# A two-layer graph network on one core: setup reordered with larger batches and two-byte compares, both node stages in five pieces, and the last stage's biases by a matmul

## The reference

```python
def reference(x, src, dst, edge_attr_128, edge_weight, kernel0, bias0, W_fwd, b_fwd, W_back, b_back, gamma, beta):
    h = relu(layernorm(x))
    # layer 0: a degree-normalised sum over edges, times a matrix
    deg = segment_sum(w, src) + 1; dinv = rsqrt(deg)
    x = x + relu(segment_sum(dinv[src] * w * dinv[dst] * (h @ kernel0)[dst], src) + dinv**2 * (h @ kernel0) + bias0)
    h = relu(layernorm(x))
    # layer 1: messages both ways along each edge, averaged per node
    agg = segment_sum(concat([h[src], edge_attr]) @ W_fwd + b_fwd, dst) \
        + segment_sum(concat([h[dst], edge_attr]) @ W_back + b_back, src)
    agg = agg / (cnt + 1e-7)                       # cnt: messages that reach the node
    return x + gamma * layernorm(leaky_relu(agg) + h) + beta
```

## Time and profile before

| what | value |
|---|---|
| median of 3 runs | 4291.05 us (4282.3 to 4295.39) |
| profiled execution | 4283.32 us, of which the span of the trace is 4281.5 us |
| busy: PE, DVE, POOL, ACT | 78%, 74%, 70%, 44% of the span |
| mean granted TensorE clock | 0.933 |

### The profile page before, as it was taken

How to read it: one execution, slowest core, us unless ns; L and a number is a source line. 1 busy time by engine, 2 the same in 40 slices (tenths; PEclk the granted TensorE clock), 3 DMA queues, 4 the chain that set the end, 5 groups by cost and what they waited for, 6 DMA issues and landing times. The chain is left out here.

```text
span 4281.5 us, 100129 instructions
## 1 busy us (share of the span) xinstructions
PE 3343.3 (78%) x30312; PEld 2791.7 (65%) x30528; DVE 3161.2 (74%) x8053; ACT 1868.7 (44%) x4498; POOL 2999.1 (70%) x1809
## 2 busy tenths in 40 slices
PE   1454699888889888889923598889888888899964
PEld 1344577777777777777813477667767776777653
DVE  6999888888888888888825776666666666677527
ACT  1031355555555555555515244444444444445523
POOL 2666588888888888888840788777777777788301
PEclk9989899999999999999966699999999999999987
DMA  9992688777788778777876455445445544555761
GB/s 174 266 236 15 136 143 143 142 133 143 135 140 142 140 135 144 138 138 142 143 153 171 81 85 84 76 77 79 81 74 78 78 80 75 79 81 85 109 133 31
DMA packets 711723, 505.09 MB, mean 118 GB/s; under 512 B 305599, under 2 KB 617342, under 8 KB 711048
## 3 DMA queue, kind: packets, MB, share of 16 engines
q0 software_dynamic: 257584, 176.81, 37.2%
q1 hardware_dynamic: 453592, 321.45, 29.3%
HBM read 284.31 MB, written 240.17 MB: 122 GB/s over the span
## 5 line engine op out<-in xcount | busy, mean ns | idle before, releaser
L1632 POOL DMA_INDIRECT gcn_sums<-shared,ds_to_i x752 | 1289.6, 1715 | 515.5 <-ACT shared L1883 297.9
L806 POOL DMA_INDIRECT gcn_sums<-fl_sums,fl_to_i x864 | 1441.3, 1668 | 287.5 <-DMA gcn_sums<-fl_sums,fl_to_i 155.8
L1838 PE MATMUL bank<-ds_counts,ds_parts 128*128 128x256 bf16 x3675 | 605.2, 278 | 0.0
L1907 ACT COPY ds_turned<-bank 128x1024 bf16<-128x1024 bf16 (+1 forms) x325 | 313.1, 963 | 615.5 <-PE bank L1823 615.5
L1034 ACT COPY fl_sums<-bank 128x256 f32<-128x256 f32 x864 | 324.7, 376 | 567.3 <-PE bank L962 503.6
L1871 ACT CAST ds_counts<-bank 128x392 bf16<-128x392 f32 x800 | 382.2, 490 | 225.7 <-PE bank L1782 213.0
L844 DVE SCALAR_TENSOR_TENSOR fl_same<-fl_key_b,fl_pat,bank 128x128 f32<-128x128 bf16 x864 | 370.4, 441 | 104.4 <-PE bank L962 85.7
L1858 PE MATMUL bank<-ds_turned,ds_now 128*128 128x512 bf16 (+1 forms) x1734 | 427.7, 377 | 11.4 <-issue 0.2
L1767 DVE TENSOR_TENSOR src_sums<-src_sums,bank 128x512 f32<-128x512 f32 (+1 forms) x325 | 213.1, 656 | 281.1 <-PE bank L1858 276.4
L1800 PE MATMUL bank<-shared 128*128 128x128 f32 x1504 | 307.7, 309 | 119.7 <-DVE attr_sums L1684 91.7
L1697 DVE SCALAR_TENSOR_TENSOR shared<-shared,ds_pat,from_me 128x128 f32<-128x128 bf16 x752 | 312.7, 442 | 108.1 <-PE bank L1802 96.4
(11 more groups left out here) (254 smaller groups left out, 6927.2 us busy)
## 6 DMA issues: line engine op xcount, KB each, us to landing
fl_attrs<-in_edge_attr SPq DMA_DIRECT2D x108, 512.0 KB, 4.8
shared<-in_edge_attr SPq DMA_DIRECT2D x186, 256.0 KB
fl_rel_b<-dst_offset SPq DMA_DIRECT2D x108, 256.0 KB
fl_key_b<-src_key SPq DMA_DIRECT2D x108, 256.0 KB
gcn_sums<-zeros SPq DMA_DIRECT2D x40, 640.0 KB
shared<-src_key SPq DMA_DIRECT2D x94, 256.0 KB, 3.9
gcn_sums<-fl_sums,fl_to_i POOLq DMA_INDIRECT x864
near<-src_float SPq DMA_DIRECT2D x1, 12892.0 KB
```

The costliest lines, as they stand in the source:

```text
L806: nc.gpsimd.indirect_dma_start(out=d.tab_gcn[j % K], out_offset=bass.IndirectOffsetOnAxis(ap=to_i[:, (GPI * kk + gi) % 4, j:j + 1], axis=0 ...
L1632: nc.gpsimd.indirect_dma_start(out=d.tab_gcn[j % K].rearrange("n (two f) -> (n two) f", two=2), out_offset=bass.IndirectOffsetOnAxis(ap=to ...
L1838: ins = nc.tensor.matmul(row_bank[:, 0:2 * P], parts[:, tile, s, :], counts[:, h, tile, :, :].rearrange("p b q -> p (b q)"), start=(tile = ...
```

## The change

Four things are changed. In the setup, the order check is put behind the first batch, a batch has `HJ = 32` chunks (the last one 16), and `SECTIONS` is written anew for that. The three compares of the search read two-byte keys on both sides in pairs, and two of the counts behind them first add halves (`fold`) before they reduce. In the two node stages everything is done in five pieces of ten tiles, each with loads, mean, deviation, root and stores of its own. In `last_nodes` the two biases come from a fifth product (`count_rows`, two rows of counts, times `bias_rows`), for which the counts are transposed by TensorE, copied by ScalarE and moved by ScalarE's own queue; the VectorE steps of three tiles are interleaved.

The setup:

```diff
-        SECTIONS = ((1, 14, "search_rows"), (14, 20, "offsets"), (20, 27, "search_edges"), (27, 33, "deviations"), (33, 42, "places"), (42, NG // 4, None))
+        SECTIONS = ((1, 7, "search_rows"), (7, 10, "offsets"), (10, 14, "search_edges"), (14, 16, "deviations"), (16, 21, "places"), (21, LAST // 2, None))
...
+            def fold(t, n):
+
+                link(nc.vector.tensor_tensor(t[:, :, 0:n // 2], t[:, :, 0:n // 2], t[:, :, n // 2:n], ALU.add))
+                link(nc.vector.tensor_tensor(t[:, :, 0:n // 4], t[:, :, 0:n // 4], t[:, :, n // 4:n // 2], ALU.add))
+                link(nc.vector.tensor_reduce(found[:], t[:, :, 0:n // 4], AX_X, ALU.add))
...
+            def check_order():
+                link(nc.vector.tensor_tensor(row_f[:, 1:EC], dst_run[:, 1:EC], dst_run[:, 0:EC - 1], ALU.subtract))
+                dve.wait_ge(heads_in, 32)
+                link(nc.vector.tensor_tensor(row_f[:, 0:1], next_first[:, 0:1], dst_run[:, EC - 1:EC], ALU.subtract))
+                link(nc.vector.tensor_reduce(bad[:, 0:1], row_f, AX_X, ALU.min))
+                nc.vector.tensor_scalar(bad[:, 0:1], bad[:, 0:1], -0.5, None, ALU.is_lt)
...
-                link(nc.vector.tensor_tensor(less1, head_bank[:, 0:HEADS].unsqueeze(1).to_broadcast([P, TILES, HEADS]), per_node(node, HEADS), ALU.is_lt))
-                link(nc.vector.tensor_reduce(found[:], less1, AX_X, ALU.add))
+                link(nc.vector.tensor_scalar(head_key[:, 0:HEADS], head_bank[:, 0:HEADS], PAT, None, ALU.add))
+                keys = in_twos(head_key[:].bitcast(BF16).unsqueeze(1).to_broadcast([P, TILES, HEADS_W]))
+                link(nc.vector.tensor_tensor(in_twos(less1), keys, node_keys(HEADS_W), ALU.is_lt))
+                fold(less1, HEADS_W)
...
             def search_rows():
                 dve.wait_ge(rows2_in, 16 * TILES)
-                link(nc.vector.tensor_tensor(less2, rows2, per_node(node_key, COARSE), ALU.is_lt))
-                link(nc.vector.tensor_reduce(found[:], less2, AX_X, ALU.add))
+                link(nc.vector.tensor_tensor(in_twos(less2), in_twos(rows2_p), node_keys(COARSE), ALU.is_lt))
+                fold(less2, COARSE)
...
-            def one_hots(i, h):
+            def one_hots(i, h, count=HJ):
                 n = 2 * i + h
-                pair = lambda t, width: t[:, bass.ds(WJ * n, WJ), :].unsqueeze(2).to_broadcast([P, WJ, width // 2, 2])
...
             one_hots(0, 0)
+            check_order()
             search_heads()
             one_hots(0, 1)
```

`gcn_nodes`, the queue, VectorE's order and ScalarE's order:

```diff
+            def load(r):
+                sp.dma_start(piece(acc, r), piece(nodes(d.g), r)).then_inc(acc_in[r], 16)
+                for k in range(K):
+                    n = r * K + k
+                    if n >= PB:
+                        sp.wait_ge(part_used, n - PB + 1)
+                    sp.dma_start(part[:, n % PB, :, :], piece(nodes(d.tab_gcn[k]), r)[:, :, 0:F]).then_inc(part_in[n % PB], 16)
...
+            load(0)
+            load(1)
+            for r in range(2, PIECES):
+                load(r)
+                store_x1(r - 2)
+                if r >= 3:
+                    store_h1(r - 3)
+            store_h1(PIECES - 3)
...
+            for r in range(PIECES):
+                add_up(r)
+                if r == 0:
+                    dve.wait_ge(w_in, 32)
+                if r > 0:
+                    deviations(r - 1)
+                products(r)
+            deviations(PIECES - 1)
...
+            for r in range(PIECES):
+                for t in tiles_of(r):
+                    if r > 0 and t % PT == 0:
+                        root(r - 1)
+                    keep_turned(t)
+                    if r > 0:
+                        bend(t - PT)
+                for t in tiles_of(r):
+                    square(t)
+            root(PIECES - 1)
+            for t in tiles_of(PIECES - 1):
+                bend(t)
```

`last_nodes`:

```diff
+            def load(r):
+                sp.dma_start(row_sums[:, r * PT * P:(r + 1) * PT * P], d.row_t[:, r * PT * P:(r + 1) * PT * P]).then_inc(row_in[r], 16)
+                sp.dma_start(piece(h1, r), piece(nodes(d.h1), r)).then_inc(h1_in[r], 16)
+                sp.dma_start(piece(x1, r), piece(nodes(d.x1), r)).then_inc(x1_in[r], 16)
...
+            load(0)
+            for m, a in enumerate((d.gamma, d.beta)):
+                sp.dma_start(per_feature[:, m, :], a.rearrange("(o f) -> o f", o=1).to_broadcast([NP, F])).then_inc(bias_in, 16)
+            for r in range(1, PIECES):
+                load(r)
+            for r in range(PIECES):
+                sp.wait_ge(out_ready, r + 1)
+                t0, t1 = r * PT, min((r + 1) * PT, WHOLE)
+                sp.dma_start(d.out[NP * t0:NP * t1, :].rearrange("(t p) f -> p t f", p=NP), agg[:, t0:t1, :]).then_inc(stored, 16)
...
+                dve.wait_ge(prod_ready, t + 1)
+                out = prod[t % B][0:NP, 0:F]
+                nc.vector.tensor_scalar(agg[:, t, :], out, per_count[:, t:t + 1], None, ALU.mult).then_inc(prod_used, 1)
...
+                nc.vector.scalar_tensor_tensor(agg[:, t, :], leaky[:, t % 2, :], 1.0, h1[:, t, :], ALU.mult, ALU.add,
+                                               accum_out=stat[:, 0, t:t + 1]).then_inc(sum_ready, 1)
...
+            def finish(r):
+                dve.wait_ge(normed, PT * (r + 1) - (TAIL if r == PIECES - 1 else 0))
+                nc.vector.tensor_tensor(piece(agg, r), piece(agg, r), per_feature[:, 0, :].unsqueeze(1).to_broadcast([NP, PT, F]), ALU.mult).then_inc(scaled, 1)
+                dve.wait_ge(scaled, r + 1)
+                dve.wait_ge(beta_added, r + 1)
+                nc.vector.tensor_tensor(piece(agg, r), piece(agg, r), piece(x1, r), ALU.add).then_inc(out_ready, 1)
...
+            dve.wait_ge(bias_in, 32)
+            for t in range(NT + 2):
+                by_count(t)
+                bend(t - 1)
+                add_up(t - 2)
+                r, at = divmod(t, PT)
+                if at == 1 and r > 0:
+                    mean(r - 1)
+                if at == 1 and r > 1:
+                    finish(r - 2)
+                if at == 6 and r > 0:
+                    variance(r - 1)
+                if at == 7 and r > 0:
+                    scale(r - 1)
...
+                    pe.wait_ge(counts_in, 64)
+                nc.tensor.matmul(out, count_rows[:, t * NP:(t + 1) * NP], bias_rows[:], start=False, stop=False)
                 pe.wait_ge(turn_copied, t + 1)
-                nc.tensor.matmul(out, turn_sb[:, t % 2, :], w[:, 0, :], start=False, stop=True).then_inc(prod_ready, 1)
+                nc.tensor.matmul(out, turn_sb[:, t % 2, :], w[:, 0, :], start=False, stop=False)
+                if t % PT == 0:
+                    pe.wait_ge(row_in[t // PT], 16)
+                nc.tensor.matmul(out, row_sums[:, t * NP:(t + 1) * NP], w[:, 3, :], start=False, stop=True).then_inc(prod_ready, 1)
...
+                nc.scalar.dma_start(count_rows[m:m + 1, :].rearrange("o (t p) -> o t p", p=P), count_t[:, m, :]).then_inc(counts_in, 16)
+                nc.scalar.dma_start(bias_rows[m:m + 1, :], b.rearrange("(o f) -> o f", o=1)).then_inc(counts_in, 16)
...
+                r, at = divmod(t, PT)
+                if r > 0 and 2 <= at <= 5:
+                    for q in range(3 * (at - 2), min(3 * (at - 2) + 3, PT)):
+                        square((r - 1) * PT + q)
+                if r > 0 and at == 6:
+                    root(r - 1)
+                if r > 0 and at >= 7:
+                    for q in range(4 * (at - 7), min(4 * (at - 7) + 4, PT)):
+                        norm((r - 1) * PT + q)
```

More of the change, by code:

```diff
@@ L1339, in _ @@
-            for r in range(2):
-                sp.wait_ge(h_ready, HT * (r + 1))
-                sp.dma_start(half(nodes(d.h1), r), half(acc, r)).then_inc(stored, 16)
-            sp.wait_ge(stored, 16 * 3)
+            load(0)
[6 more added lines that the diff above has]
+            store_h1(PIECES - 3)
+            store_x1(PIECES - 2)
+            store_h1(PIECES - 2)
@@ new lines, in _ @@
+            for t in range(NT + 2):
[11 more added lines that the diff above has]
+                    scale(r - 1)
+            last = PIECES - 1
+            variance(last)
@@ L2159, in _ @@
+            scale(last)
+            dve.wait_ge(scale_ready, PIECES)
+            for t in tiles_of(last)[PT - TAIL:]:
+                here = nc.vector.tensor_scalar(agg[:, t, :], agg[:, t, :], stat[:, 1, t:t + 1], stat[:, 0, t:t + 1], ALU.mult, ALU.add)
+            link(here)
+            finish(last)
         @block.tensor
```

372 lines of the change are left out of this document (185 added, 187 removed).

## The result

The changed kernel takes 4252.2 us (4248.3 to 4253.9, 4 runs) where the kernel before took 4287.8: a ratio of 0.991, interval 0.9894 to 0.9926. That is 36 us saved; the forecast was 102. The profiled execution has a span of 4250.4 us, 31.1 less than before.

What follows compares the result with a forecast made beforehand. Stages were read separately: setup bound by VectorE, `gcn_nodes` by successive phases, `last_nodes` by waiting for `h1`, then VectorE's dependent steps. Savings of 40 + 25 + 37 = 102 us gave a 4179.5 us span, 4186 forecast, range 4158 to 4216.

Steps and rivals of the forecast that it cites:

- Clock: Rival: stalls in each piece of `last_nodes` drop TensorE to 1.2 GHz; 71 us saved, 4217; chance 0.15.
- nine passes of which the bias product adds two: 1.22 us: `last_nodes`: TensorE's time per tile, up from 1.00 us because of the bias product.
- ScalarE's order: `last_nodes`: ScalarE's list of copies, squares, root and outputs makes a piece 17.7 us where TensorE alone needs 12.2.
- its 50 fetches take 77.3 us: Setup: GpSimd's first set of fetches keeps its earlier pace beside the larger batches, leaving a 6.5 us wait.
- the length of a batch: Setup: a batch of 32 takes 5.82 us against 3.08 for one of 16, saving 17 us.
- All three covers: Setup: VectorE's work against three fetch sets: a 6.5 us wait, 10 us of cover, then 81.5 us that just fits.
- Roots: `last_nodes`: eight more roots on ScalarE cost nothing beyond their own 0.25 us each.
- Table switches: Rival: a 1.28 us table load on either side of eight additional roots; 82 us saved, 4206; chance 0.03.
- Large batches lose the fast rate: Rival in setup: a batch of 32 takes 11.2 us at 1.04 ns an element; 4456, slower; chance 0.02.
- Transfers bound setup: Rival: edge records pushed 50 us back, VectorE stands some 22 us; 80 us saved, 4208; chance 0.05.
- I expect it to shift as a block: Stretches between the changed stages, some 3530 us: untouched, so they keep their length.
- VectorE's waits at more than one hook: Setup: named sign of a wrong forecast; one wait of about 6 us was expected, at the first `search_rows`.

Runs made afterwards that it cites:

- e1: Changed kernel with the count and bias rows padded by 126 rows of zeros, so the bias product has 128 rows; 4200.8 us, ratio 0.9797 to the kernel before.
- e5: Changed kernel with setup batches of 16 chunks and the bias product padded to 128 rows, zeros written by VectorE and GpSimd; 4176.1 us, 0.9746 of the kernel before.
- e3: Changed kernel with setup's batches back at 16 chunks, new order and two-byte compares kept; 4235.0 us, ratio 0.9878 to the kernel before.
- e16: Kernel before with g multiplied and stored in five pieces instead of two; 4343.0 us, one run.

## Why the prediction was wrong

The sum was 102, the two traces give 31. The 71 between them are 66 from `last_nodes` and 20.5 from setup, less 2.3 more gained in `gcn_nodes` and 13.5 in the untouched stretches. The median, 4252, lies above the range of 4158 to 4216. That range also had an error of its own: Clock, with a chance of 0.15, was priced at 4217, just outside it.

- **`last_nodes`: the step that failed is "nine passes of which the bias product adds two: 1.22 us".** I priced a product of two rows like one of 128. On the chip it costs another 0.62 us a tile at the lower clock, and the clock stays there, so a tile takes 2.94. Both vanish with the 126 rows of zeros (e1). The stage was TensorE's, as forecast, but at that price. The padded product (e5) gives back what I had described: 1.23 us a tile where nothing waits, pieces of 20.0, 17.9 and 17.0 us against my 17.7, and 119.6 us for the stage against my 114; that it starts 4 us later accounts for most of the rest (VectorE's first step comes 16.6 us behind the first load, not 13). ScalarE's order costs what I counted.
- **The rival Clock had the right state for the wrong reason.** I let stalls of up to 4 us drop the clock, and thought it unlikely since the one drop in the rows followed 16 us without work. That its 4217 is nearer to the result than the forecast's 4186 is luck: the clock never rose at all, in a loop whose longest stall is 1.23 us, and 23 us a piece was too little: three pieces took 92.1 us on ScalarE's timeline, 30.7 each.
- **Setup: the step that failed is "its 50 fetches take 77.3 us".** Order check (18.9), compares (9.9) and the length of a batch came out as costed: without the large batches setup saves 29.4 (e3). I called the fetches independent of VectorE because they ran beside the batches; that they took two to a batch exactly, 1.54 in 3.08, was in the rows I read the earlier trace rows. The new waits are 35 us where I allowed 9.5; setup lost 20.5 of these 25.5, and where the other 5 came back stays open. All three covers that I counted (6.5 short, 10 over, "just fits") used the same pace, 77.3 or 78.3 us a set.
- **`gcn_nodes`** was right in its steps: 16.3 us a piece, a slow and a fast half in each burst.
- **Roots** cost their own 0.21 us; the whole trace has two table loads, as before, and none beside a root. Table switches is ruled out, and so are Large batches lose the fast rate (5.81 us) and Transfers bound setup (the records are issued at 249.4 us, before at 252.2, and none of VectorE's waits is for them).
- **"I expect it to shift as a block"** was wrong by 17.5 us in one stretch. Before, that stretch is 1790.8 and 1794.6 us; after any edit ahead of it that I tried it is 1771 to 1783. Without this, 18 us would be left of the change. About half of the changed kernel's gain thus owes nothing to what the change was made for: twelve memsets off the path give nearly as much in that stretch. I had named this as a sign of being wrong, and VectorE's waits at more than one hook as the other; both came.

What stays open: what makes that stretch longer in the kernel before, and whether it is the same thing that stands at the loops in e16; and why the clock rises with 64 rows, late, and not with 32.

## What to carry to other kernels

Give a small product beside full ones the same number of rows, by zeros if need be, and look at the granted clock of the whole stage afterwards and not only at its busy share: 100% busy at 0.50 is the worst of both. Where GpSimd issues transfers beside VectorE, the length of VectorE's instructions sets their pace, so a larger batch may cost more than its fixed part saves. And before a gain or loss of 10 to 20 us in a long program is put down to an edit, profile one with a meaningless edit at the same place.

## What the runs showed that I had not expected

- A product of 2 or 32 rows among products of 128: starts 0.57, 0.72 and 0.59 us apart instead of 0.42, and a granted clock of 0.50 through the whole loop, 50 us of TensorE without a pause among it. With 64 rows 0.31, 0.42 and 0.32 instead of 0.22, and a clock that rises only after 14 us without a pause; with 128 rows none of it.
- A fetch of GpSimd takes 0.95 us with VectorE idle; beside it, it ends 0.9 us behind the start of one of VectorE's instructions, whichever comes next: 1.54 us a fetch beside instructions of 0.5 to 1.2 us, 1.94 beside 0.9 to 2.3.
- Twelve memsets off the path made setup 16 us longer and a stretch that begins 1.9 ms later 11 to 15 us shorter; three more stores and multiplications, 76 longer and 10 to 14 shorter (one profile each).
